# Fewer unread decay products, one wait more on GpSimd, and other places for the gated stage's guests

## The chip, the cores and the metric

The kernel runs on one core of a Trainium2 chip. The metric is the device time in microseconds (us) of one execution. TensorE (PE) multiplies matrices, VectorE (DVE), ScalarE (ACT) and GpSimd (POOL) work element by element, and SyncE (SP) issues DMAs. Each engine runs its instructions in order, and engines wait for each other by semaphores.

## What is computed

Four layers over 16 batches of 256 tokens with 128 channels. Each adds `layernorm(f(layernorm(x)))` to x:

```
x = x + _layernorm(_L0_attn_ref(_layernorm(x), ...))   # softmax attention, 16 heads of 8
x = x + _layernorm(_L0_ffn_ref(_layernorm(x), ...))    # attention, then 8 experts (top 2) and a shared one
x = x + _layernorm(_L1_attn_ref(_layernorm(x), W))     # power attention with decay
x = x + _layernorm(_L1_ffn_ref(_layernorm(x), ...))    # 7 capped experts
```

In the second layer a token's output is the shared expert's plus two chosen experts', each weighted. The third is the one with the decay:

```
log_G = jnp.cumsum(jax.nn.log_sigmoid(...), axis=1)
Tm = DEG * jnp.log(jnp.abs(S) + EPS) + jnp.log(jnp.float32(scale))   # DEG = 2
Z = Tm + log_G[..., :, None] - log_G[..., None, :]
P = jnp.exp(Z - Z_rowmax);  O = P @ V;  y = O / sum(P)
```

## The kernel before

Four stages run one after the other in one program: softmax attention (twice, up to about 500 us of the span), the gated experts (500 to 668), the power attention (668 to 955) and the capped experts with their routing (955 to 1102).

**The gated stage** (`gated_layer`) goes over 62 units n of 256 rows; `ORDER` says which unit is one of the shared expert (16 of them) and which is of rows sorted by expert (46). For a unit PE computes the gate and up products (`ggate_ps`, `gup_ps`, L2346), ACT the silu of the gate (`gsg`, L2430), DVE the product of both (`gprod`, L2645), and PE, one to four units later, the down product (`gdown_ps`, L2318). DVE adds a shared unit's result to XB (`add_shared`, L2573); ACT copies a sorted one's to `gob` (L2399), and SP stores it to DRAM (`mixed`). `down` for unit x waits, because `gdown_ps` has two banks, until unit x-2 was taken (`released`). `finished(kind, n)` lists the units whose result DVE or ACT takes at step n, ahead of the product; `DOWNS` lists the down products that PE makes at steps 4 and 5.

GpSimd scatters rows to their sorted places (L2175) by 32 indirect DMAs for the second half of the rows, waits for stores, and gathers results back (`ggot`, L2187) by 8 indirect DMAs for each block of 512 tokens; there are 8 blocks b. A block then passes through `add0` and `add1` (4 DVE instructions each, L2586, which weigh the gathered rows into XB), `moments` (L2598, L2602, L2603), a root on GpSimd (`out_root`, L2193, at the places in `ROOTS`), `shift` (L2607), `rows` on ACT (4 activations, L2405; `first` and `second` are two of them each), and `added` (L2613), the sum into X. Two dictionaries from step to calls, the guests, say after which unit each engine does these; the first work of the power stage (T, QK, V, CS for batches 0 and 1, `moments`, `gates`, `rows`, `softplus`) stands in the same dictionaries. `s_sum` counts finished additions, two a block, and `gated.EARLY` is 6.

**The power stage** (`power_layer`) goes over steps t, one for each batch and then some to run out, with 8 units u in each; n = 8t + u. For a unit PE fills a bank with decays (`decay_ps`, from `late` and then from M, L1560) and score banks (L1564, L1578), DVE takes the score's absolute value (`A`, L1419), ACT takes exp of the decay (`E`, L1235) and the square of A (`PT`, L1223), GpSimd multiplies both in `PT` (`multiply`, L993) two units later, and PE multiplies by V (L1597). E has 4 buffers, so ACT's exp of unit n waits for the multiply of n-4. The order on every engine is written out by (t, u). In `decays`, L1543 starts the accumulation; the products of L1542 before it go to the same bank, and L1543 (start=True) overwrites them, so nobody reads them. There is one of them in each unit for t < 10, none for t from 10 to 13, and two for t = 14 and 15.

Blocks 4 to 7 are gathered and added while the power stage begins: `add0(4)` at (0, 1), `add1(4)` at (0, 3), `add0(5)` at (0, 7), `add1(5)` at (1, 0). ACT waits for `s_sum` of 12 before the square of unit 9.

Of the kernel before, what the change touches and what calls it, by code (L numbers as in the profile page):

```python
# [41 lines left out]
NB, S, D = 16, 256, 128  # L42
# [791 lines left out]
def power_layer(nc, low, weighted_in, top, take, X, cst, cstb, QK, Vx, w, Y, chosen, router, bias, yd, wi, wo, gated, dram):  # L834
# [7 lines left out]
    with ExitStack() as ctx:  # L842
# [235 lines left out]
        def gpsimd(pool, guests):  # L1078
# [432 lines left out]
        def tensor(pe, guests):  # L1511
# [92 lines left out]
            for t in STEPS:  # L1604
                for u in range(NU):
                    n = NU * t + u
# [378 lines left out]
def gated_layer(nc, big, small, temps, got_late, hTf, sg, prod, take, X, XB, cst, split, down_w, norm, lg, soft,  # L1985
# [33 lines left out]
    def turned_at(n):  # L2019
        kind, i = ORDER[n]  # L2020
        return turn_of(n) if kind == "sorted" or i % 2 == 0 else None

    with ExitStack() as ctx:
# [616 lines left out]
        def vector(dve, guests):  # L2640
# [333 lines left out]
def build(nc, dram, out):  # L2974
    with ExitStack() as ctx:
# [21 lines left out]
        with ExitStack() as c1:  # L2997
# [54 lines left out]
            def _(pool):  # L3052
# [25 lines left out]
                gated.gpsimd(pool, {**{("fixed", k): guest("fixed", k) for k in range(7)},  # L3078
                                    ("gather", 2, 2): several(guest("root", 0), guest("norm0", 0), guest("norm1", 0)),
                                    ("gather", 2, 7): guest("root", 1),  # L3080
                                    ("gather", 3, 1): several(guest("norm0", 1), guest("norm1", 1)),
                                    "end": several(guest("root", 2), guest("norm0", 2), guest("norm1", 2))})
# [10 lines left out]
            def _(act):  # L3093
# [9 lines left out]
                def rows(b):  # L3103
                    return lambda: gated.tail_scalar(act, "rows", b)

                def several(*calls):
                    return lambda: [call() for call in calls]
# [4 lines left out]
                soft.scalar(act, heads)  # L3112
                gated.scalar(act, {39: rows(0), 45: rows(1), 49: rows(2), 44: guest("T", 0), 46: guest("QK", 0),
                                   48: guest("V", 0), 50: guest("T", 1), 52: guest("QK", 1),
                                   54: several(guest("V", 1), guest("softplus", 0)), 56: guest("CS", 0),
                                   57: rows(3), 59: guest("CS", 1)})
                def half(part, b):
                    return lambda: gated.tail_scalar(act, part, b)

                after = {(0, 0): guest("factors", 0), (1, 0): rows(4)}  # L3120
# [5 lines left out]
            def _(dve):  # L3126
# [9 lines left out]
                def several(*calls):  # L3136
# [8 lines left out]
                soft.vector(dve, heads)  # L3145
                gated.vector(dve, {36: tail(("add0", 0)), 37: tail(("add1", 0), ("moments", 0)), 39: tail(("shift", 0)),
                                   40: several(tail(("added", 0)), guest("moments", 0)), 41: tail(("add0", 1)),
                                   42: tail(("add1", 1), ("moments", 1)), 43: guest("moments", 1), 44: tail(("shift", 1)),
                                   45: tail(("added", 1)), 46: several(guest("QK", 0), guest("moments", 2)),
                                   47: tail(("add0", 2)), 48: tail(("add1", 2), ("moments", 2)), 49: tail(("shift", 2)),  # L3150
                                   50: tail(("added", 2)), 51: tail(("add0", 3)), 52: guest("QK", 1),
                                   53: tail(("add1", 3), ("moments", 3)), 55: guest("gates", 0), 56: tail(("shift", 3)),
                                   57: several(guest("rows", 0), guest("gates", 1)),
                                   58: tail(("added", 3)), 59: guest("rows", 1),
                                   61: tail(("shared", gated.UNITS - 3))})
                after = {(0, 0): tail(("shared", gated.UNITS - 2)), (0, 1): tail(("add0", 4)),
# [57 lines left out]
```

## Time and profile before

| | us |
|---|---|
| median of 3 runs (lowest, highest) | 1105.17 (1102.54, 1108.28) |
| profiled execution, its own time | 1104.22 |
| its span, first to last instruction | 1102.3 |
| busy: PE / DVE / ACT / POOL | 992.7 / 850.8 / 774.9 / 637.9 |
| mean granted TensorE clock, share of full | 0.962 |

A busy share is an average over four stages with different limits. PE is listed busy from a matmul's start to its modelled end, so two pipelined matmuls overlap in it.

### The profile page before, as it was taken

To read this page: it belongs to the slowest core of one execution; us is meant where nothing else is said; L and a number is where in the kernel's file an instruction comes from. 1 tells how busy PE (TensorE), PEld (TensorE's weight loads), DVE (VectorE), ACT (ScalarE), POOL (GpSimd) and SP (SyncE) were. 2 spreads that over 40 slices of the span, in tenths; PEclk is the share of its full clock that TensorE was granted. 3 is DMA by queue.
4 is the path that set the end of the run, shared out by engine and by line. 5 is a ranking of instruction groups with operands and counts; after the bars stand their busy time and mean duration, and the time that the engine had idled before them with its cause. 6 is when DMAs were issued, how large, how long until landed. Compare 5 with 4: busy or idle time off the path is not lost. (4 is left out here: it accounts for less than half of the span.)

```text
span 1102.3 us, 30949 instructions
## 1 busy us (share of the span) xinstructions
PE 992.7 (90%) x10503; PEld 586.9 (53%) x10503; DVE 850.8 (77%) x2252; ACT 774.9 (70%) x1760; POOL 637.9 (58%) x710
## 2 busy tenths in 40 slices
PE   4899999999999988988999998999999999848975
PEld 2344444444444443436998875555555565534752
DVE  3789999999999998954756767888989987772324
ACT  1578888888888877884554665788888998642405
POOL 4235544555443333760476838799888887526753
PEclk9999999999999999998999998999999999858988
DMA  5022222211111111220444421112121121141227
GB/s 133 26 58 77 77 73 77 77 55 40 41 41 40 41 33 43 59 70 20 132 124 132 134 75 41 48 43 66 44 61 32 36 58 52 40 164 41 53 74 198
DMA packets 114423, 75.24 MB, mean 68 GB/s; under 512 B 21335, under 2 KB 107808, under 8 KB 114272
## 3 DMA queue, kind: packets, MB, share of 16 engines
q1 hardware_dynamic: 105840, 54.68, 18.2%
q0 software_dynamic: 7744, 18.13, 5.5%
q8 instruction: 90, 1.47, 0.6%
q14 instruction: 61, 0.50, 0.2%
q10 hardware_dynamic: 688, 0.46, 0.1%
HBM read 26.75 MB, written 26.51 MB: 48 GB/s over the span
## 5 line engine op out<-in xcount | busy, mean ns | idle before, releaser
L637 DVE TENSOR_REDUCE mxsS<-scoreS 128x2 f32<-128x512 f32 x512 | 327.7, 685 | 40.9 <-PE scoreS L779 37.2
L519 ACT ACTIVATE PTS<-stS 128x512 f32<-128x512 f32 x512 | 284.1, 595 | 55.4 <-PE stS L783 54.2
L779 PE MATMUL scoreS<-QK 31*128 31x256 f16 x1024 | 171.6, 280 | 30.6 <-DVE mxsS L637 16.5
L993 POOL TENSOR_TENSOR PTP<-PTP,EP 128x512 f32<-128x512 f32 x128 | 163.3, 1280 | 38.7 <-ACT PTP L1223 37.7
L783 PE MATMUL stS<-QK 32*128 32x256 f16 x1024 | 169.4, 278 | 2.3 <-ACT PTS L519 2.3
L701 PE MATMUL pvS<-PTS,Vx 128*32 128x256 f32 x2048 | 142.0, 396 | 0.4 <-ACT PTS L519 0.2
L779 PEld LDWEIGHTS scoreS<-QK 31*128 31x128 f16 x1024 | 52.7, 93 | 152.6 <-DVE mxsS L637 105.5
L1419 DVE TENSOR_SCALAR AP<-score_psP 128x768 int32<-128x768 int32 x128 | 121.7, 951 | 12.1 <-PE score_psP L1578 10.6
L1223 ACT ACTIVATE PTP<-AP,epsP 128x768 f32<-128x768 f32 x128 | 118.9, 929 | 6.8 <-DVE AP L1419 6.5
L392 POOL TENSOR_TENSOR rsS<-veS,halfS 128x2 f32<-128x2 f32 (+1 forms) x32 | 33.0, 1031 | 154.0 <-DVE veS L605 87.1
L1235 ACT ACTIVATE EP<-decay_psP 128x512 f32<-128x512 f32 x128 | 75.7, 592 | 29.1 <-PE decay_psP L1560 27.4
L2175 POOL DMA_INDIRECT sorted<-gy,gidx x64 | 62.0, 969 | 41.5 <-DVE gowner L2537 22.8
L701 PEld LDWEIGHTS pvS<-PTS,Vx 128*32 128x32 f32 x2048 | 54.5, 111 | 51.0 <-issue 23.0
L2318 PE MATMUL gdown_ps<-down_w,gprod 128*128 (+1 forms) x496 | 65.7, 276 | 3.4 <-DVE XB L2573 3.1
L2318 PEld LDWEIGHTS gdown_ps<-down_w,gprod 128*128 128x128 f32 x496 | 60.1, 192 | 5.3 <-issue 4.4
L2645 DVE TENSOR_TENSOR gprod<-gsg,gup_ps 128x512 f32<-128x512 f32 x62 | 42.5, 686 | 22.2 <-ACT gsg L2430 10.9
L2187 POOL DMA_INDIRECT ggot<-mixed,gidx x48 | 46.7, 973 | 21.7 <-issue 13.3
L2367 ACT ACTIVATE ghTs<-gturn_ps,norm 128x256 f16<-128x256 f32 x46 | 21.8, 473 | 50.3 <-PE gturn_ps L2257 49.5
L783 PEld LDWEIGHTS stS<-QK 32*128 32x128 f16 x1024 | 51.9, 93 | 6.2 <-ACT PTS L519 3.1
L1560 PEld LDWEIGHTS decay_psP<-MP 32*128 32x128 bf16 x512 | 28.5, 93 | 48.6 <-issue 44.1
L398 POOL TENSOR_SCALAR yS<-X,mvS,rsS 128x128 f32<-128x128 f32 x64 | 50.6, 797 | 1.7
L1564 PE MATMUL score_psP<-QK 31*128 31x128 f16 x512 | 50.6, 218 | 0.0
(399 smaller groups left out, 2310.7 us busy)
## 6 DMA issues: line engine op xcount, KB each, us to landing
QK<-HLS SPq DMA_DIRECT2D x384, 32.0 KB
QK<-HLP SPq DMA_DIRECT2D x192, 32.0 KB
gsin<-sorted SPq DMA_DIRECT2D x46, 128.0 KB
mixed<-gob SPq DMA_DIRECT2D x46, 128.0 KB
sorted<-ggot POOLq DMA_DIRECT2D x22, 256.0 KB, 2.7
expert_outputs<-tzero SPq DMA_DIRECT2D x8, 512.0 KB
cgot<-expert_outputs SPq DMA_DIRECT2D x16, 256.0 KB, 5.4
tokens<-XB SPq DMA_DIRECT2D x16, 128.0 KB
```

The costliest lines, as they stand in the source:

```text
L398: last = pool.tensor_scalar(y[:, c, :], rows_of(X, b)[c], mv[:, c, 0:1], rs[:, kind, c:c + 1], ALU.subtract, ALU.mult)
L519: act.activation(PT[:, n % NPT, :], st_ps[:, (NS * t + n) % 3, :], ACT.Exp, scale=SCALE).then_inc(s_exp, 1)
L637: dve.tensor_reduce(mxs[:, u // 4, :, at], score_ps[:, n % 2, :].rearrange("p (c s) -> p c s", c=TC), AX.X, ALU.max).then_inc(s_max, 1)
L701: last = pe.matmul(pv_ps[32 * j:32 * j + 32, q], Vx[:, t % 3, c, 4 * g + j, :], PT[:, (4 * g + (j ^ 2)) % NPT, S * c:S * c + S], start=(c ...
L779: scored = pe.matmul(score_ps[:, k, cols], QK[part, new, g, 0, rows], QK[part, new, g, 1, :], start=True, stop=True)
L783: turned = pe.matmul(st_ps[:, (NS * t + n) % 3, cols], QK[part, old, g, 1, rows], QK[part, old, g, 0, :], start=True, stop=True)
L993: eng.tensor_tensor(w, w, E[:, n % NE, :], ALU.mult).then_inc(s_wd if n % NU in MULT_BY_DVE else s_wp, 1)
L1223: act.activation(PT[:, n % NW, :], A[:, n % NA, :], ACT.Square, bias=eps[:, 0:1]).then_inc(s_sq, 1)
L1235: act.activation(E[:, n % NE, :], decay_ps[:, n % 2, :], ACT.Exp).then_inc(s_taken, 1)
L1419: dve.tensor_scalar(A[:, n % NA, :].bitcast(I32), score_ps[:, n % 2 * WU:n % 2 * WU + WU].bitcast(I32), 0x7FFFFFFF, None, ALU.bitwise_and) ...
L2175: pool.indirect_dma_start(tables[h], bass.IndirectOffsetOnAxis(ap=idx[h][:, c, t:t + 1], axis=0), y[:, tiles[h].start + t, :], None).then_ ...
L2318: last = pe.matmul(down_ps[:, x % 2, t * D:(t + 1) * D], prod[:, x % NPROD, c * SLOTS + t * P:c * SLOTS + (t + 1) * P], down_flat[:, colum ...
```

## The change

It does four things. In the power stage the unread product remains in steps 0 and 1 (one) and 15 (two), and goes in steps 2 to 9 (one in each of 64 units) and 14 (two in each of 8). GpSimd waits at (1, 0), ahead of its multiply of unit 6, until `s_sum` is 12. In the gated stage units 0 to 3 are taken by DVE right behind the products of units 4 and 5 instead of ahead of those of 5 and 6. And the guests of units 35 to 61, with GpSimd's order of fixed rows, scatters, gathers and roots, are laid out anew.

```
@@ power_layer, gpsimd
                 for u in range(NU):
                     n = NU * t + u - 2
+                    if (t, u) == (1, 0):
+                        pool.wait_ge(gated.s_sum, 2 * gated.EARLY)
                     if 0 <= n < NU * NB and n % NU not in MULT_BY_DVE:
                         multiply(pool, n)
@@ power_layer, decays
-                for _ in range(AGAIN if t >= NB - 2 else t < 10):
+                for _ in range(AGAIN if t == END else t < 2):
                     pe.matmul(decay_ps[:, n % 2, :], cstb[:, 0:P], late, start=True, stop=True)
@@ gated_layer
-        ROOTS = ((1, 4), (2, 6), (3, 6))
+        ROOTS = ((1, 6), (2, 7), (3, 7))
         def gpsimd(pool, guests):
             scaled_rows(pool, NBLK - 1)
+            for k in range(7):
+                guests["fixed", k]()
             for k in range(2 * len(tiles[1])):
                 scatter(pool, 1, k)
-            for k in range(7):
-                guests["fixed", k]()
...
-            return [x for x in ({5: (0, 1), 6: (2, 3)}.get(n, (n - 3,) if n > 6 else ())) if ORDER[x][0] == kind]
+            return [n - 3] if n > 6 and ORDER[n - 3][0] == kind else []
...
                 product(n)
+                for x in DOWNS.get(n, ()):
+                    add_shared(dve, x)
@@ build, scalar
-                gated.scalar(act, {39: rows(0), 45: rows(1), 49: rows(2), 44: guest("T", 0), 46: guest("QK", 0),
...
-                                   57: rows(3), 59: guest("CS", 1)})
+                gated.scalar(act, {39: half("first", 0), 40: half("second", 0), 44: guest("T", 0), 45: half("first", 1),
...
+                                   56: guest("CS", 0), 58: half("first", 3), 59: guest("CS", 1), 60: half("second", 3)})
@@ build, vector
-                gated.vector(dve, {36: tail(("add0", 0)), 37: tail(("add1", 0), ("moments", 0)), 39: tail(("shift", 0)),
...
-                                   53: tail(("add1", 3), ("moments", 3)), 55: guest("gates", 0), 56: tail(("shift", 3)),
+                gated.vector(dve, {35: tail(("add0", 0)), 36: tail(("add1", 0)), 37: tail(("moments", 0)),
...
+                                   55: several(guest("gates", 0), tail(("added", 2))), 56: tail(("moments", 3)),
```

ACT's halves stand at units 39 and 40, 45 and 46, 53 and 55, 58 and 60. On GpSimd the guests of the power stage move from (gather, 2, 2), (2, 7) and (3, 1) to (2, 5) and (3, 2).

DVE, gated stage, from the product of unit 4. Before (`gprod` the product, `ghTs` the low half of a later unit's rows, `gm` to `gone` the first four steps of choosing experts, `XB<-gdown_ps` two shared units added):

```order
L2645 TENSOR_TENSOR gprod<-gsg,gup_ps 128x512
L2450 SCALAR_TENSOR_TENSOR ghTs<-gturn_ps,norm,ghTs 128x256
L2482 TENSOR_REDUCE gm<-lg 128x16
L2483 TENSOR_TENSOR gpr_121<-lg,gm 128x128
L2484 SCALAR_TENSOR_TENSOR gsc<-gpr_121,cst 128x128
L2485 TENSOR_REDUCE gone<-gsc 128x16
L2573 SCALAR_TENSOR_TENSOR XB<-gdown_ps,XB 128x256 x2
L2645 TENSOR_TENSOR gprod<-gsg,gup_ps 128x512
```

And after:

```order
L2647 TENSOR_TENSOR gprod<-gsg,gup_ps 128x512
L2575 SCALAR_TENSOR_TENSOR XB<-gdown_ps,XB 128x256 x2
L2452 SCALAR_TENSOR_TENSOR ghTs<-gturn_ps,norm,ghTs 128x256
L2484 TENSOR_REDUCE gm<-lg 128x16
L2485 TENSOR_TENSOR gpr_121<-lg,gm 128x128
L2486 SCALAR_TENSOR_TENSOR gsc<-gpr_121,cst 128x128
L2487 TENSOR_REDUCE gone<-gsc 128x16
L2647 TENSOR_TENSOR gprod<-gsg,gup_ps 128x512
```

The two additions moved up past five instructions; the same holds one unit later.

DVE, gated stage, block 0 behind the product of unit 36. Before:

```order
L2586 SCALAR_TENSOR_TENSOR XB<-ggot,gW,XB 128x128 x4
L2645 TENSOR_TENSOR gprod<-gsg,gup_ps 128x512
L2450 SCALAR_TENSOR_TENSOR ghTs<-gturn_ps,norm,ghTs 128x256
L2586 SCALAR_TENSOR_TENSOR XB<-ggot,gW,XB 128x128 x4
L2598 BN_STATS gstats<-XB 128x6 x4
L2602 BN_AGGR gmv<-gstats 128x2 x4
L2603 TENSOR_SCALAR gve<-gmv 128x4
L2645 TENSOR_TENSOR gprod<-gsg,gup_ps 128x512
```

And after, from the first additions, now behind unit 35:

```order
L2588 SCALAR_TENSOR_TENSOR XB<-ggot,gW,XB 128x128 x4
L2647 TENSOR_TENSOR gprod<-gsg,gup_ps 128x512
L2452 SCALAR_TENSOR_TENSOR ghTs<-gturn_ps,norm,ghTs 128x256
L2588 SCALAR_TENSOR_TENSOR XB<-ggot,gW,XB 128x128 x4
L2647 TENSOR_TENSOR gprod<-gsg,gup_ps 128x512
L2452 SCALAR_TENSOR_TENSOR ghTs<-gturn_ps,norm,ghTs 128x256
L2600 BN_STATS gstats<-XB 128x6 x4
L2604 BN_AGGR gmv<-gstats 128x2 x4
L2605 TENSOR_SCALAR gve<-gmv 128x4
L2647 TENSOR_TENSOR gprod<-gsg,gup_ps 128x512
```

A product now stands between the second additions and the moments.

GpSimd, gated stage, from the last scaled rows (`MP`, `VkP`: fixed rows of the power stage; `grs`: root of a block; `rsP`, `yP`: guests of the power stage). Before:

```order
L2175 DMA sorted<-gy,gidx_109 5888x128 x32
L1054 CAST MP<-cst 128x4x256 x4
L1058 MEMSET VkP 128x3x256 x2
L2187 DMA ggot<-mixed,gidx_108 128x128 x13
L2193 TENSOR_TENSOR grs<-gve,ghalf 128x4
L2187 DMA ggot<-mixed,gidx_108 128x128 x6
```

And after:

```order
L1054 CAST MP<-cst 128x4x256 x4
L1058 MEMSET VkP 128x3x256 x2
L2177 DMA sorted<-gy,gidx_109 5888x128 x32
L2189 DMA ggot<-mixed,gidx_108 128x128 x15
L2195 TENSOR_TENSOR grs<-gve,ghalf 128x4
L2189 DMA ggot<-mixed,gidx_108 128x128 x7
```

The fixed rows moved ahead of the scatters, and block 0's root behind two more gathers.

## Rows read from the trace of the kernel before

**Rows 1.** Windows, power stage: stretch and length, busy us (count), clock, DMA.

```profile
670.80:692.40 21.60, 16.60 (x164) 8.38 (x166) 18.16 (x41) 13.36 (x24) 18.13 (x17) 0.84 0.14 37
...
726.50:743.80 17.30, 16.98 (x223) 9.46 (x224) 16.27 (x47) 15.29 (x35) 16.16 (x17) 1.00 0.20 50
762.10:781.00 18.90, 18.45 (x238) 10.35 (x238) 17.18 (x47) 15.99 (x35) 16.63 (x16) 1.00 0.21 53
798.40:816.70 18.30, 17.69 (x229) 10.09 (x228) 15.56 (x40) 16.60 (x39) 17.19 (x16) 1.00 0.22 57
...
852.90:870.10 17.20, 15.92 (x221) 9.95 (x220) 15.82 (x40) 16.19 (x38) 14.56 (x15) 1.00 0.13 34
870.10:886.30 16.20, 16.09 (x221) 9.95 (x220) 14.66 (x40) 14.79 (x35) 13.10 (x13) 1.00 0.14 36
...
918.90:936.40 17.50, 17.50 (x227) 9.48 (x228) 13.88 (x33) 13.51 (x27) 12.32 (x11) 1.00 0.22 62
```

**Rows 2.** Source view of L1419: count, ns min/median/max, first and last start.

```profile
L1419 DVE TENSOR_SCALAR AP<-score_psP x128: 935/950/959, 670.8 to 950.7; 128x768 int32<-128x768 int32 x128
```

**Rows 3.** Timeline of PE, step 1: start us, us, engine line op.

```profile
701.40 0.39 PE L1542 MATMUL decay_psP<-cstb 128*128 128x512 bf16 x1
701.62 0.38 PE L1543 MATMUL decay_psP<-cstb 128*128 128x512 bf16 x1
```

**Rows 4.** Timeline of PE, gated units 4 to 7: idle before in brackets.

```profile
511.32 1.95 PE L2318 MATMUL gdown_ps<-down_w,gprod 128*128 128x128 f32 x16
...
516.29 2.02 PE L2318 MATMUL gdown_ps<-down_w,gprod 128*128 128x128 f32 x16 [1.49 <-DVE XB L2573]
...
521.43 1.15 PE L2318 MATMUL gdown_ps<-down_w,gprod 128*128 x8 [1.59 <-DVE XB L2573]
```

**Rows 5.** Timeline of DVE, gated unit 4 to the product of unit 5.

```profile
512.51 0.69 DVE L2645 TENSOR_TENSOR gprod<-gsg,gup_ps 128x512 f32<-128x512 f32 x1 [0.85 <-PE gdown_ps L2318]
...
515.72 0.76 DVE L2573 SCALAR_TENSOR_TENSOR XB<-gdown_ps,XB 128x256 f32<-128x256 f32 x2
```

**Rows 6.** Source view of L2645 in two windows, 584:597 and 596.4:648.

```profile
L2645 DVE TENSOR_TENSOR gprod<-gsg,gup_ps x6: 686/689/689, 584.4 to 596.5; 128x512 f32<-128x512 f32 x6
...
L2645 DVE TENSOR_TENSOR gprod<-gsg,gup_ps x19: 677/686/690, 596.5 to 647.8; 128x512 f32<-128x512 f32 x19
```

**Rows 7.** Timeline, gated stage: a product of DVE, ACT's rows of block 0.

```profile
637.46 0.69 DVE L2645 TENSOR_TENSOR gprod<-gsg,gup_ps 128x512 f32<-128x512 f32 x1 [2.46 <-ACT gsg L2430]
...
606.15 1.65 ACT L2405 ACTIVATE gtmp<-XB,gnm,grs 128x128 f32<-128x128 f32 x4 [0.62 <-DVE gnm L2607]
```

**Rows 8.** Timeline of GpSimd, gated stage and its end.

```profile
536.09 1.06 POOL L2175 DMA_INDIRECT sorted<-gy,gidx  x1 [22.82 <-DVE gowner L2537]
...
576.42 3.98 POOL L1054 CAST MP<-cst 128x1024 bf16<-128x1024 f32 x4
...
647.90 1.03 POOL L2193 TENSOR_TENSOR grs<-gve,ghalf 128x4 f32<-128x4 f32 x1 [9.46 <-DVE gve L2603]
656.73 1.10 POOL L2187 DMA_INDIRECT ggot<-mixed,gidx  x1 [7.80 <-DMA mixed<-gob]
...
676.62 2.50 POOL L993 TENSOR_TENSOR PTP<-PTP,EP 128x512 f32<-128x512 f32 x2
...
689.73 1.27 POOL L993 TENSOR_TENSOR PTP<-PTP,EP 128x512 f32<-128x512 f32 x1
```

**Rows 9.** Timeline of DVE, steps 0 and 1: the additions of blocks 4 and 5.

```profile
673.20 1.13 DVE L2586 SCALAR_TENSOR_TENSOR XB<-ggot,gW,XB 128x128 f32<-128x128 f32 x4
...
676.93 4.78 DVE L2586 SCALAR_TENSOR_TENSOR XB<-ggot,gW,XB 128x128 f32<-128x128 f32 x4
...
693.28 1.46 DVE L2586 SCALAR_TENSOR_TENSOR XB<-ggot,gW,XB 128x128 f32<-128x128 f32 x4
```

**Rows 10.** Timeline of ACT, exp of units 4 and 10.

```profile
677.99 0.60 ACT L1235 ACTIVATE EP<-decay_psP 128x512 f32<-128x512 f32 x1 [0.74 <-POOL PTP L993]
...
695.38 0.58 ACT L1235 ACTIVATE EP<-decay_psP 128x512 f32<-128x512 f32 x1
```

More of the change, by code:

```diff
@@ L3078, in _ @@
                 gated.gpsimd(pool, {**{("fixed", k): guest("fixed", k) for k in range(7)},
-                                    ("gather", 2, 2): several(guest("root", 0), guest("norm0", 0), guest("norm1", 0)),
-                                    ("gather", 2, 7): guest("root", 1),
-                                    ("gather", 3, 1): several(guest("norm0", 1), guest("norm1", 1)),
+                                    ("gather", 2, 5): several(guest("root", 0), guest("norm0", 0), guest("norm1", 0)),
+                                    ("gather", 3, 2): several(guest("root", 1), guest("norm0", 1), guest("norm1", 1)),
                                     "end": several(guest("root", 2), guest("norm0", 2), guest("norm1", 2))})
@@ L3104, in rows, with half @@
                     return lambda: gated.tail_scalar(act, "rows", b)
+                def half(part, b):
+                    return lambda: gated.tail_scalar(act, part, b)
                 def several(*calls):
@@ L3112, in _ @@
                 soft.scalar(act, heads)
-                gated.scalar(act, {39: rows(0), 45: rows(1), 49: rows(2), 44: guest("T", 0), 46: guest("QK", 0),
-                                   48: guest("V", 0), 50: guest("T", 1), 52: guest("QK", 1),
-                                   54: several(guest("V", 1), guest("softplus", 0)), 56: guest("CS", 0),
-                                   57: rows(3), 59: guest("CS", 1)})
-                def half(part, b):
-                    return lambda: gated.tail_scalar(act, part, b)
+                gated.scalar(act, {39: half("first", 0), 40: half("second", 0), 44: guest("T", 0), 45: half("first", 1),
+                                   46: several(half("second", 1), guest("QK", 0)), 48: guest("V", 0), 50: guest("T", 1),
+                                   52: guest("QK", 1), 53: half("first", 2),
+                                   54: several(guest("V", 1), guest("softplus", 0)), 55: half("second", 2),
+                                   56: guest("CS", 0), 58: half("first", 3), 59: guest("CS", 1), 60: half("second", 3)})
                 after = {(0, 0): guest("factors", 0), (1, 0): rows(4)}
@@ L3145, in _ @@
                 soft.vector(dve, heads)
-                gated.vector(dve, {36: tail(("add0", 0)), 37: tail(("add1", 0), ("moments", 0)), 39: tail(("shift", 0)),
[L3147 to L3151, printed above, removed]
-                                   53: tail(("add1", 3), ("moments", 3)), 55: guest("gates", 0), 56: tail(("shift", 3)),
-                                   57: several(guest("rows", 0), guest("gates", 1)),
-                                   58: tail(("added", 3)), 59: guest("rows", 1),
-                                   61: tail(("shared", gated.UNITS - 3))})
+                gated.vector(dve, {35: tail(("add0", 0)), 36: tail(("add1", 0)), 37: tail(("moments", 0)),
+                                   38: tail(("shift", 0)), 39: tail(("add0", 1)), 40: tail(("added", 0)), 41: guest("moments", 0),
+                                   42: tail(("add1", 1)), 43: tail(("moments", 1)),
+                                   44: tail(("shift", 1)), 45: guest("moments", 1), 46: guest("QK", 0),
+                                   47: tail(("added", 1)), 48: guest("moments", 2), 49: tail(("add0", 2)),
+                                   50: tail(("add1", 2)), 51: tail(("moments", 2)), 52: guest("QK", 1),
+                                   53: tail(("shift", 2), ("add0", 3)), 54: tail(("add1", 3)),
+                                   55: several(guest("gates", 0), tail(("added", 2))), 56: tail(("moments", 3)),
+                                   57: several(guest("rows", 0), guest("gates", 1), tail(("shift", 3))),
+                                   59: guest("rows", 1),
+                                   61: tail(("added", 3), ("shared", gated.UNITS - 3))})
                 after = {(0, 0): tail(("shared", gated.UNITS - 2)), (0, 1): tail(("add0", 4)),
```

## The prediction

> **What bounds the kernel now.** I read the windows by stage first, then the waits of each engine in the stages that the change touches, then the timelines at the waits that ended last. The chain of waits at the kernel's end lies in the capped experts, behind all of this; what is gained ahead of it moves it as a whole, so each stage is read for itself.
>
> In the power stage I cut the windows at the start of every eighth L1419, so that one window is one step; there are 128 of them from 670.8 to 950.7 us [rows 2]. A step takes 16.2 to 18.9 us. PE is listed busy for nearly all of it (16.09 of 16.20 in step 11), but DVE and ACT are close: in step 3 DVE has 16.27 of 17.30, in step 5 17.18 of 18.90 [rows 1]. PE holds most units, DVE those in which it has additions or moments to do besides. A microsecond taken from PE is thus worth less than one.
>
> In the gated stage DVE's products show the pace: 5 units from 584.4 to 596.5, 2.42 us each, with PE busy all the time, then 18 units from 596.5 to 647.8, 2.85 us each [rows 6]. Two places lie outside that pace: PE idle 1.49 and 1.59 us in units 5 and 6 [rows 4].
>
> The power stage's first step takes 21.6 us at a clock of 0.84 [rows 1], because DVE, GpSimd and PE stumble over the last gathers.
>
> **The unread products.** 64 + 16 = 80 matmuls go. One costs PE 0.22 us from its start to the next [rows 3], so 17.6 us if PE were all that counts: one end. The other is nothing, if DVE and ACT hold every unit. Steps with and without one stand in the same trace. Step 7 (one a unit) and step 10 (none) have the same work beside it, the second half of a block's rows on ACT and its sum on DVE, except for two gathers on GpSimd: 18.3 against 17.2 us [rows 1], 1.1 for the 1.8 us of PE taken out. Steps 4 and 7: 2 x 1.1 = 2.2. Steps 3, 6 and 9 carry a block's moments: DVE has 16.27 in 17.30 [rows 1] against 14.66 in 16.20 in step 11, and step 11 shows that DVE loses 1.5 us a step to waits even without the product. 16.3 + 0.7 to 1.5 is 17.0 to 17.8, so the gain is 0.3 at most: 3 x 0.3 = 0.9. Steps 5 and 8 carry the additions: 17.18 of DVE and the 1.4 us that it waits in step 10 (17.20 less 15.82) give 18.6, against 18.9; with some of these waits gone, 18.2. I take 0.7 each, 1.4. Step 2 lies between these kinds: 0.5. Step 14 loses two a unit: 17.5 against 16.2 in step 11, though DVE has less to do in it (13.88 against 14.66) [rows 1]; I take 1.1. Sum 6.1; by bounds 2.5 (only steps 4, 7 and part of 14) to 9.
>
> **Units 4 to 6 of the gated stage.** The down products of units 0 and 1 run on PE from 511.32 to 513.27 [rows 4]. DVE could add them then, but its product of unit 4 ends at 513.2 and four steps of choosing follow; the additions come at 515.72 [rows 5]. PE has to wait for them with its next down product, until 516.29, and once more until 521.43 [rows 4]. After the change the additions follow the product: 513.3 to 514.0, before PE asks: its wait of 1.49 us ended at 516.29, so it asked at 514.8. For units 2 and 3 the product of unit 5 now no longer waits for 0.76 us of additions, and PE asks about 3 us later. Both waits go: 3.1. What is late next is DVE itself: its chain of choosing ends the ranks, and the first scatter waits for it 22.82 us [rows 8]; it moves up with PE, as does everything that PE paces up to unit 35.
>
> Against it stands what GpSimd now does in the same time. The fixed rows, with 3.98 us of CAST [rows 8], run from 513.3 on, not at 576.4. In the trace two of DVE's instructions with two SBUF operands, of the four in one addition, stretched under GpSimd's multiplies, 4.78 for 1.13 us [rows 9]; the CASTs have one operand, and no row has such a DVE instruction beside them. If they block, up to four of choosing's instructions wait until about 517.4, and of the 3.1 us 1.2 are left. If not, 3.1. I take 2.6, nearer to the row without any hold. The fixed rows' own 5.4 us cost nothing in the idle 22.82, and gain nothing: the gathers behind them wait for stores that PE paces.
>
> The Trainium skill says of this (SBUF — State Buffer, section "SBUF: two separate sides") that VectorE and GpSimd share a port pair as an exclusive lock, also for a VectorE instruction with two SBUF inputs against any GpSimd instruction that reads SBUF. By that the CASTs block and the term would be 1.2; the 4.78 us agree with the lock, and no run here shows it for a CAST.
>
> **The guests of units 35 to 61.** 18 units took 51.3 us, and at the pace ahead of them 43.6. The power stage's T, QK and V for two batches are PE's own work; from their durations I estimate 2.2 us a set, 4.3 for both. So 3.4 us are lost where guests bunch: DVE's product waits 2.46 us for ACT (one of two such waits), behind four of ACT's rows, 1.65 us in one piece [rows 7]. Halves and one kind of guest a unit break that up. All of it is 3.4, nothing is 0, and worse is possible in units 53 to 60, where ACT gets 0.8 us in 53 and again in 55, beside the softplus: up to 1 us lost. I take 2.0, a little over the middle.
>
> **The entry to the power stage.** Block 3's moments go from unit 53 to 56, so its root on GpSimd, at 647.90 before, comes after them, by this count at about 657 to 659 in the old times. The 16 gathers of blocks 4 and 5 stand behind it; they began at 656.73, held by a store, and the first multiply came right behind them at 676.62 [rows 8]. They begin 1 to 3.5 us later. ACT's exp of unit 4 already waited 0.74 us for that multiply [rows 10], so this lands on the path, up to 3.5. In return the additions of block 4, which took 4.78 instead of 1.13 us under the multiplies [rows 9], may get through before them: up to 3.6 back. The new wait holds the multiply of unit 6, at 689.73 before [rows 8], until block 5's additions end at 693.28 + 1.46 = 694.7 [rows 9]: 5 us. Behind it on GpSimd stand the multiplies of 7 and 8 and a gather; ACT's exp of unit 10 waits for the held multiply, which would end at 696.0, 0.6 us later than the exp began [rows 10]. With GpSimd late already, the wait costs less. Together between 3 gained and 4 lost; I take 0.7 lost.
>
> **Sum.** 6.1 + 2.6 + 2.0 - 0.7 = 10.0 us, from the profiled execution's 1104.2: 1094.2. That execution lies 0.95 under the median of the runs (1105.17), within their scatter; I give 1094.5.
>
> **Rivals.** First, *DVE holds the steps*. Steps 3, 5, 6, 8 and 9 give nothing, and waits for DVE take PE's place: 2.5 instead of 6.1. For it: DVE's 16.3 of 17.3 us. Against: the 1.1 us between steps 7 and 10, both with additional work. Time 1098.1.
>
> Second, *GpSimd comes late*. The root behind unit 56 puts the gathers 3.5 us back, none of DVE's blocking goes, and the wait in step 1 is paid in full: 4 lost at the entry, 1097.5. For it: the multiply right behind the gathers, and exp waiting for it. Against: E's four buffers, and that most of the 4.78 was blocking.
>
> Third, on the other side, *the clock falls*. PE's clock was at its upper level (2.4 GHz) in the windows from step 2 on, and its mean in step 0, where PE waited long for DVE, 0.84 [rows 1]. Without the unread products PE has less to do in steps held by DVE, most of all 5 and 8. At 1.2 GHz the 16.1 us of PE in a step become 32, so one step costs 16 us: from 0.6 of a step on the gain is used up, and with one the time is 1110. Against: steps 10 to 13 have none of them and kept 1.00, step 10 with 15.92 of 17.20 [rows 1]. The Trainium skill has the rule behind it (TensorE: Matmul & The Clock Gate, Part 1): the throttled state is the default, and activity releases it.
>
> **Chances.** Forecast 0.62, DVE 0.14, GpSimd late 0.15, clock 0.05, the rest 0.04 for the gated stage's layout turning out worse (1100). What a measurement of this kernel tells from no change is about 0.5%, 5.5 us: faster means under 1099.6. Of the forecast nearly all lies there, of the first two rivals some three quarters: 0.61 + 0.11 + 0.11 = 0.83, which I lower to 0.80 for what I don't see; same 0.14, slower 0.06. The range, 1088.5 to 1100.5, reaches at the upper end past both milder rivals and at the lower to bounds of 9, 3.1, 3.4 and nothing lost.
>
> **What would show it.** In the profile after: step windows 4 and 7 at 17.2 to 17.4, 14 at 16.2 to 16.5, and 3, 6, 9 at about 17 with DVE the engine waited for; clock 1.00 in all of them. No wait of `gdown_ps` for XB in units 5 and 6, and unit 14's product some 2.6 us earlier. Under 2.75 us a unit from 36 to 54. The first gather of block 4 one to three us behind the store that it waited for, and GpSimd idle ahead of the multiply of unit 6. Wrong would be steps 4 and 7 above 18, a clock under 1.00 in steps 2 to 14, or a first step above 24 us.

## The result

The changed kernel took 1110.32 us in the median of 19 runs (1102.86 to 1114.67, and one of 1452.34 us at a granted clock of 0.559, which the comparison leaves out), the kernel before 1104.00 beside it (19 runs). The ratio is 1.004, 95% interval 1.0023 to 1.0056: some 4 us slower (the two medians lie 6.3 us apart), where the prediction had said 10 faster. The profiled execution took 1113.14 us, 3 above the median, span 1111.2, mean granted TensorE clock 0.940 where it was 0.962.

The steps of the power stage tell where the time went. Windows of the kernel after, one step each (0, 1, 2, 3, 4, 5, 6, 7, 8, 9, and 14); columns as in [rows 1]:

```profile
668.60:688.50 19.90, 16.22 (x173) 8.29 (x172) 16.56 (x42) 13.09 (x24) 17.83 (x17) 0.91 0.17 45
688.50:709.00 20.50, 19.51 (x188) 10.29 (x188) 14.46 (x32) 14.89 (x31) 16.38 (x14) 0.75 0.10 26
709.00:724.30 15.30, 15.20 (x215) 9.30 (x214) 13.85 (x34) 13.79 (x30) 14.23 (x14) 1.00 0.22 56
724.30:744.20 19.90, 18.27 (x215) 10.96 (x214) 16.32 (x49) 16.27 (x36) 18.47 (x18) 0.83 0.20 50
744.20:761.40 17.20, 15.97 (x221) 9.92 (x220) 15.75 (x39) 15.60 (x36) 15.29 (x15) 1.00 0.20 50
761.40:781.00 19.60, 17.93 (x256) 11.00 (x255) 18.84 (x48) 16.94 (x37) 18.57 (x17) 1.00 0.23 58
781.00:801.50 20.50, 18.75 (x186) 11.18 (x186) 16.47 (x49) 14.63 (x33) 14.30 (x14) 0.75 0.17 46
801.50:820.30 18.80, 17.55 (x221) 11.08 (x220) 15.99 (x41) 16.65 (x39) 17.73 (x17) 0.91 0.22 56
820.30:839.90 19.60, 17.96 (x256) 11.02 (x255) 18.83 (x48) 16.70 (x36) 15.49 (x14) 1.00 0.18 45
839.90:863.90 24.00, 22.96 (x186) 13.45 (x186) 16.79 (x49) 15.63 (x35) 13.63 (x13) 0.57 0.10 25
...
929.80:945.20 15.40, 14.47 (x213) 8.62 (x213) 13.69 (x33) 13.87 (x28) 11.92 (x12) 1.00 0.27 75
```

Against [rows 1], step 4 shortened as forecast (17.2), and step 14 by more (17.5 to 15.4). But steps 3, 6, 7 and 9 ran partly at TensorE's lower level (1.2 GHz): a mean of 0.57 over 24.0 us means 20.6 us at half. Steps 2 to 9 took 154.9 us, before 143.1; PE starts fewer matmuls and is listed busy longer (step 3: 215 for 223, 18.27 us for 16.98 [rows 1]). And steps 5 and 8, which kept 1.00, got longer without their product: 19.6 us where step 5 took 18.9 [rows 1], with 18.84 us of DVE for 17.18.

Why is seen at the end of step 5. Timelines of the kernel after there, of DVE, GpSimd and PE:

```profile
778.48 0.17 DVE L1312 SCALAR_TENSOR_TENSOR lgP<-misc_aP,geP 128x32 f32<-128x32 f32 x1
778.58 2.51 DVE L2588 SCALAR_TENSOR_TENSOR XB<-ggot_late,gW,XB 128x128 f32<-128x128 f32 x2
781.01 0.94 DVE L1421 TENSOR_SCALAR AP<-score_psP 128x768 int32<-128x768 int32 x1
```

```profile
778.38 2.55 POOL L993 TENSOR_TENSOR PTP<-PTP,EP 128x512 f32<-128x512 f32 x2
```

```profile
782.01 0.28 PE L1580 MATMUL score_psP<-QK 31*128 31x128 f16 x2 [1.77 <-DVE AP L1421]
```

The same place in the kernel before, DVE and GpSimd:

```profile
780.13 0.92 DVE L2586 SCALAR_TENSOR_TENSOR XB<-ggot_late,gW,XB 128x128 f32<-128x128 f32 x2
```

```profile
779.36 1.28 POOL L993 TENSOR_TENSOR PTP<-PTP,EP 128x512 f32<-128x512 f32 x1
781.04 1.28 POOL L993 TENSOR_TENSOR PTP<-PTP,EP 128x512 f32<-128x512 f32 x1 [0.40 <-ACT PTP L1223]
```

With the product PE set the pace, and ACT's squares came 0.4 us late to GpSimd. In that gap DVE's two additions got through: they met only the end of the first multiply and took 0.92 us. Without the product the multiplies run back to back, the additions lie under them and take 2.51, DVE's next pass over the scores is late, PE waits 1.77 us for it, and the next window is the one at 0.75 (behind step 8: 0.57).

The parts ahead of the power stage came about as forecast. In the kernel after, PE's down products of units 4 to 6 don't wait, where they waited 1.49 and 1.59 us [rows 4]:

```profile
512.91 1.95 PE L2320 MATMUL gdown_ps<-down_w,gprod 128*128 128x128 f32 x16
...
516.22 1.95 PE L2320 MATMUL gdown_ps<-down_w,gprod 128*128 128x128 f32 x16
...
519.73 1.15 PE L2320 MATMUL gdown_ps<-down_w,gprod 128*128 x8
```

and the source view of DVE's products from unit 36 to 54 answers to [rows 6]:

```profile
L2647 DVE TENSOR_TENSOR gprod<-gsg,gup_ps x19: 675/686/689, 595.8 to 644.9; 128x512 f32<-128x512 f32 x19
```

49.1 us for 18 units, 2.73 each, before 2.85.

### The profile page after: what moved, and what is told of

Read it like the earlier page. It is cut to its first block and busy times, and to the rows that moved or that the text cites. A ratio compares the mean times of both kernels' runs of the same rounds, so it can differ in the third digit from the quotient of the medians.

```text
span 1111.2 us, 30790 instructions
## 1 busy us (share of the span) xinstructions
PE 996.3 (90%) x10423; PEld 596.5 (54%) x10423; DVE 853.1 (77%) x2252; ACT 776.2 (70%) x1760; POOL 637.5 (57%) x710
## 5 line engine op out<-in xcount | busy, mean ns | idle before, releaser
L1566 PE MATMUL score_psP<-QK 31*128 31x128 f16 x512 | 53.0, 226 | 0.0
L1562 PE MATMUL decay_psP<-MP 32*128 32x128 bf16 x512 | 53.0, 226 | 0.0
L1545 PE MATMUL decay_psP<-cstb 128*128 128x512 bf16 x128 | 52.7, 412 | 0.0
```

The costliest lines, as they stand in the source:

```text
L1562: decay = pe.matmul(decay_ps[:, n % 2, o:o + P], M[band, t % 2, g, 1, rows], M[band, t % 2, g, 0, rows], start=False, stop=(k == 1 and c = ...
```

## The experiments

All ran beside the kernel before, whose median stayed between 1103.9 and 1105.5; ratios are to it, with their 95% intervals. A ratio is not the quotient of the two medians; the two ways differ by up to 2.5 us, so differences of 2 us between experiments say little. "Wait theory" in the expectations stands for a fall of the clock set off by single waits of PE, "load theory" for one set off by too little work in a step. "Kept in" and "gone in" speak of the steps that have the unread product, which nobody reads: no output depends on it.

**Products and layout apart.** Four kernels: the kernel before with the condition

```
-                for _ in range(AGAIN if t >= NB - 2 else t < 10):
+                for _ in range(AGAIN if t == END else t < 2):
```

and nothing else (e1); the changed kernel without that line (e2); and the same two with step 14's products alone gone (e3, e4: `AGAIN if t == END else t < 10`).

> The kernel before with the unread products alone taken out (steps 2 to 9 and 14). Clock theory (without them PE's clock falls in steps that DVE holds): the granted clock falls in two or more of steps 3, 6, 9, these steps take 19.5 to 24 us in place of 17.3, mean clock 0.94 to 0.955, ratio 1.004 to 1.012. Rival (the slower time comes from the new GpSimd wait and the late root, not from the products): no fall after step 1, steps 4 and 7 at 17.3, ratio 0.993 to 0.997.

> The changed kernel with the unread products as before, so only the gated stage's layout and the GpSimd wait are new. Clock theory: no fall of the clock from step 2 to 14, first product of the power stage some 3.5 us earlier, ratio 0.993 to 0.998. Rival (GpSimd wait and late root): steps 0 and 1 together 2 us or more longer than the 38.9 of before, ratio 1.002 to 1.006.

> The kernel before with the products of step 14 alone taken out (steps 0 to 9 keep one a unit). Clock theory: no DVE-held step is touched, so no fall, step 14 at 15.5 to 16.3 in place of 17.4, ratio 0.998 to 0.9995. Rival (any unread product keeps the clock up): a fall in step 14 or 15, step 14 over 18, ratio over 1.001.

> The changed kernel with the products kept in steps 0 to 9 and gone only in step 14. Clock theory: gains of the gated stage and of step 14 add, ratio 0.991 to 0.997. Rival (GpSimd wait): ratio 1.000 to 1.005.

Measured: e1 1118.06 us, 1.0104 [1.0069, 1.0140]; e2 1097.23, 0.9932 [0.9901, 0.9962]; e3 1101.56, 0.9972 [0.9948, 0.9996]; e4 1097.50, 0.9926 [0.9898, 0.9955]. All four ratios lie where the clock theory had them (e3 a little below); but e2 and e3 have a fall of 3.4 us in step 10, where the expectation of e2 had none. So the products' removal costs 11 to 12 us in either layout (13 by the medians), and the rest of the change gains 7.5. Windows of e1, steps 5 and 6, in which nothing but the products differs from before:

```profile
757.90:777.50 19.60, 17.95 (x256) 11.00 (x255) 18.84 (x48) 16.94 (x37) 18.57 (x17) 1.00 0.23 58
777.50:801.50 24.00, 22.98 (x186) 13.49 (x186) 16.68 (x49) 15.73 (x35) 15.68 (x15) 0.57 0.16 43
```

and the same steps in e2:

```profile
753.00:771.90 18.90, 18.45 (x238) 10.35 (x238) 17.16 (x47) 15.99 (x35) 16.61 (x16) 1.00 0.20 55
771.90:789.20 17.30, 16.99 (x223) 9.80 (x220) 16.29 (x49) 15.00 (x34) 15.64 (x15) 1.00 0.21 55
```

**Is it the wait, or too little work?** In e10 all products stay, and DVE does its first pass for units 48 and 72 (first of steps 6 and 9) three times (arguments of the calls left out below). e9, e5 and e6 are the kernel before with products gone in two or three steps (`t < 10 and t not in (5, 8)` and so on).

```
+                        for k in range(2 if n in (48, 72) else 0):
+                            dve.tensor_scalar(A[:, n % NA, :].bitcast(I32), ...).then_inc(s_twice, 1)
+                            dve.wait_ge(s_twice, 2 * (n // 72) + k + 1)
                         dve.tensor_scalar(A[:, n % NA, :].bitcast(I32), ...).then_inc(s_abs, 1)
```

> The kernel before with all its unread products, and VectorE's first pass over the scores of the first unit of steps 6 and 9 done three times in place of once, the first two read by nobody: a wait of about 1.6 us for TensorE at the start of these two steps, made by nothing else. Wait theory in its strict form (a wait alone does it): the clock falls to half behind both for 10 to 20 us, ratio 1.008 to 1.015. If it takes the wait and steps that are short of work together: the clock stays, 2 x 1.9 us more, ratio 1.003 to 1.004.

> The kernel before, the unread product left out in steps 5 and 8 alone. Wait theory: in both, VectorE's two additions into XB behind lgP come to lie under GpSimd's multiply (1.23 and 1.36 us for 0.66 and 0.34), the step is 19.6 us for 18.9, TensorE waits 1.77 us at the start of the next, and the granted clock falls to half there though steps 6 and 9 have their products: 0.7 and about 6 us more, each twice, ratio 1.008 to 1.013. Load theory: the additions and the wait are there, but steps 6 and 9 with their products keep the clock: 1.4 us more, ratio 0.999 to 1.003.

> The kernel before, the unread product left out in steps 2, 4 and 7 alone. Wait theory: the clock is held at half only where TensorE has just waited 1.2 us or more in front of a far score for VectorE's first pass; in these steps the only such waits are of 1.2 us (steps 4 and 7, as with the products all gone), none longer, so no long fall. The steps shorten as in the run with the products gone, 16.8 to 15.4, 18.3 to 17.3 and 18.3 to 17.3: 3.5 us less, ratio 0.996 to 0.999. Load theory (TensorE has too little work in a step without the product, wherever it is): a fall in or behind each of the three, ratio 1.003 to 1.01.

> The kernel before, the unread product left out in steps 3, 6 and 9 alone, the steps that showed 20 us at half clock when it was gone everywhere. Wait theory: the waits of 1.77 us at the start of steps 6 and 9 come from the step ahead of each (5 and 8, which keep their product here), so they don't occur and steps 6 and 9 stay at full clock, 16.9 to 17.4 us; step 3 may keep a wait of 1.26 us and a fall of 3.4 us (+1.5 us). Ratio 0.998 to 1.002. Load theory: steps 6 and 9 run at half clock for 20 us again, 6.6 us more each, ratio 1.008 to 1.013.

e10: 1116.21 us, 1.0126 [1.0096, 1.0156], 14 us for two waits (12 by the medians). In its profile steps 5 and 8, at whose ends the waits stand, took 2 us more each, and steps 6 and 9, at the lower clock, 2.7 and 5.6 more. Timeline of PE at the two places, and windows of the steps they stand in (6 and 9):

```profile
782.13 0.22 PE L1584 MATMUL score_psP<-QK 31*128 31x128 f16 x1 [1.69 <-DVE AP L1425]
...
841.38 0.28 PE L1584 MATMUL score_psP<-QK 31*128 31x128 f16 x2 [1.67 <-DVE AP L1425]
```

```profile
781.10:801.20 20.10, 18.69 (x193) 10.51 (x194) 16.71 (x48) 14.41 (x34) 14.00 (x15) 0.83 0.16 45
...
840.40:863.30 22.90, 21.53 (x192) 11.57 (x192) 16.59 (x48) 14.66 (x33) 12.31 (x12) 0.70 0.08 21
```

With every product in place a wait of 1.7 us was followed by the fall, both times: a wait alone is enough. e9: 1106.20, 1.0009 [0.9984, 1.0033]. Its windows of steps 8 and 9, and PE at the start of step 9:

```profile
818.60:838.20 19.60, 18.31 (x257) 11.01 (x256) 18.84 (x48) 16.79 (x36) 16.23 (x15) 1.00 0.19 51
838.20:855.40 17.20, 15.77 (x192) 9.03 (x192) 16.19 (x49) 14.39 (x33) 12.31 (x12) 1.00 0.11 29
```

```profile
839.17 0.22 PE L1578 MATMUL score_psP<-QK 31*128 31x128 f16 x1 [1.35 <-DVE AP L1419]
```

The additions are stretched again (18.84 of DVE), but two of step 9's own products stand on PE ahead of that score (at 834.06 and 835.73) and fill 0.4 of the 1.77 us; with 1.35 left the clock held. A fall of 3.4 us stood in step 5, behind waits of only 0.42 and 0.48 us. Here my expectation of a fall missed, and the number is that of the load theory; e10 shows that full steps don't hold the clock against a wait of 1.7 us, but the fall in step 5 has no such wait. e5: 1101.62, 0.9971 [0.9955, 0.9988]; steps 2, 4 and 7 at 15.6, 17.5 and 17.5 us, clock 1.00, as the wait theory had it. e6: 1100.69, 0.9971 [0.9948, 0.9994], no fall in its three steps (17.3, 17.2 and 17.2 us); in its profile steps 2 to 9 together shorten by 0.6, so its measured gain of 3 us is larger than its steps account for.

**Only steps 5 and 8 put back.** e11 is the changed kernel, e14 the kernel before, both with this condition (in e14 the last step is written `NB - 1`, the same)

```
+                for _ in range(AGAIN if t == END else t < 2 or t in (5, 8)):
```

> The changed kernel, its unread product put back in steps 5 and 8 alone (so in steps 0, 1, 5, 8 and 15). Theory (a wait of TensorE of about 1.7 us sets off the fall, stretched additions of steps 5 and 8 make the wait): the additions are 0.66 and 0.34 us again, no wait above 1.4 us stands between steps 3 and 9, no fall of 10 us or more between them; the time is that of the kernel with products kept but in 14 (1097.5) less about 3 us, 1094, ratio 0.988 to 0.992. Rival (too few products as such): falls stay in steps 3, 6, 7 and 9 and the ratio is 1.000 or more.

> The kernel before with the products of the changed kernel and those of steps 5 and 8 as well; nothing moved. Against the run with the products gone in 2 to 9 and 14 (1.0104) it differs by the 16 products of steps 5 and 8 alone. Theory as for the run above: 0.988 to 0.994, 15 to 20 us under it with 16 instructions more. Rival (too few products as such): 1.005 or more.

e11: 1099.42, 0.9943 [0.9921, 0.9964]; e14: 1103.78, 0.9986 [0.9962, 1.0009]. Against e1 (1.0104) e14 issues 16 matmuls more and is about 13 us quicker. DVE's additions at the end of step 5 in e11, and its windows of steps 3, 5, 6, 8 and 9:

```profile
772.04 0.93 DVE L2588 SCALAR_TENSOR_TENSOR XB<-ggot_late,gW,XB 128x128 f32<-128x128 f32 x2
```

```profile
716.60:736.60 20.00, 18.24 (x216) 11.04 (x215) 16.76 (x50) 16.22 (x36) 18.67 (x18) 0.83 0.19 50
754.00:772.90 18.90, 18.45 (x240) 10.54 (x239) 17.16 (x47) 16.26 (x37) 16.89 (x16) 1.00 0.23 56
772.90:791.30 18.40, 16.84 (x211) 10.67 (x210) 15.81 (x50) 15.54 (x36) 16.80 (x16) 0.91 0.23 58
810.70:832.00 21.30, 20.86 (x240) 11.29 (x240) 17.25 (x47) 15.59 (x36) 14.00 (x13) 0.87 0.15 39
832.00:849.20 17.20, 15.48 (x211) 9.51 (x210) 16.20 (x50) 14.70 (x34) 13.58 (x13) 1.00 0.13 32
```

The additions are back at 0.93 and the falls of 20 us are gone. But shorter ones stay, of 6.8 and 10.2 us by PE's waits of 1.38 (step 3) and 1.23 us (step 7), and one of 3.4 in step 6 behind a wait of only 0.80: the forecast of 0.988 to 0.992 was too good. So was that of e14, 0.988 to 0.994: its profile has falls of 13.7 us from step 3 on and three of 3.4, in steps 4, 6 and 9. Of the rival it is true that falls stay, but not its time.

**Which steps can be without.** The changed kernel with products gone in 4, 7 and 14 (e15), in 4, 6, 7, 9 and 14 (e18), and kept to step 10 (e17); conditions `t < 10 and t not in (4, 7)`, `t < 4 or t in (5, 8)`, `t < 11`.

> The changed kernel with the unread product left out in steps 4, 7 and 14 alone. Steps 4 and 7 are held by TensorE, and without their product they took 17.3 to 17.5 us for 18.3 with waits of 1.15 to 1.23 us. Wait theory (only waits of some 1.5 us and more reliably set off a fall): no fall of 6 us or more between steps 2 and 9, and 1.7 to 2.0 us less than with 14 alone (0.9926): ratio 0.990 to 0.992. Load theory: a fall in or behind steps 4 and 7 gives it back: 0.993 to 0.996.

> The changed kernel with the unread product left out in steps 4, 6, 7, 9 and 14: against the run with only 5 and 8 put back (0.9943) it keeps steps 2 and 3 as well. Wait theory: the wait of 1.3 us in step 3 and its 6.8 us at half clock (step 3 19.9 for 17.3) need steps 2 and 3 both without products, so they go; steps 6 and 9 may still show a fall of 3.4 us. 2.6 us less and 1.5 more for step 2: ratio 0.991 to 0.994. Load theory: falls remain in steps 6, 7 and 9 and nothing is won, 0.994 to 0.997.

> The changed kernel with its unread product in steps 0 to 10 and 15, so in step 10 as well, which had none in any kernel so far and in most profiled executions shows a wait of 1.22 us and 3.4 us at half clock (18.7 us for 17.3). Wait theory: the products fill the time, the wait goes, the step takes 17.3 us with its clock full in every execution: 1 us under the kernel that has them in 0 to 9 and 15 (0.9926), ratio 0.991 to 0.993. Rival (the products only take TensorE's time): 1 us above, 0.9935.

e15: 1098.33, 0.9926 [0.9887, 0.9964]. e18: 1098.32, 0.9927 [0.9899, 0.9955]. e17: 1098.55, 0.9950 [0.9926, 0.9975]. e18 came within its forecast; e15 and e17 came out above theirs, e15 with a fall of 3.4 us in step 7, and the intervals of both reach down into the forecast. No version is told from e4 (0.9926). Windows of e15, steps 4, 7 and 10, of e18, step 3, and of e17, step 10:

```profile
740.20:757.70 17.50, 16.26 (x222) 9.98 (x222) 16.07 (x41) 16.48 (x39) 16.88 (x17) 1.00 0.21 55
793.90:812.90 19.00, 17.78 (x222) 11.18 (x222) 16.04 (x40) 16.70 (x39) 17.66 (x17) 0.91 0.22 56
849.10:869.30 20.20, 18.90 (x221) 11.73 (x220) 15.96 (x40) 16.98 (x39) 15.67 (x15) 0.83 0.14 36
```

```profile
722.80:740.00 17.20, 16.88 (x222) 9.44 (x222) 16.19 (x47) 15.18 (x34) 16.19 (x16) 1.00 0.19 51
```

```profile
846.30:864.40 18.10, 17.49 (x228) 10.06 (x226) 15.50 (x40) 16.41 (x38) 14.94 (x14) 1.00 0.13 34
```

Steps 4 and 7 of e15 have nearly the same work; one kept its clock, the other lost 1.5 us, behind waits of 1.16 and 1.15. With steps 2 and 3 kept in e18, step 3's wait and fall are gone, as expected; falls of 3.4 us stay in steps 4, 6 and 9. In e17 a product in step 10 removes the wait of 1.22 us and the clock holds, but the step takes 0.8 us more than the 17.2 of [rows 1]: by the median it wins nothing.

**The entry and the CASTs.** e13 is e11 without GpSimd's new wait, e16 the kernel before with that wait alone, e12 e11 with the fixed rows back behind the scatters.

```
                     n = NU * t + u - 2
+                    if (t, u) == (1, 0):
+                        pool.wait_ge(gated.s_sum, 2 * gated.EARLY)
```

> The first kernel of this call without GpSimd's wait for the additions at the start of the second step. Theory: the wait costs 0.9 us of GpSimd's time and nothing of the end; without it the multiply of unit 6 and the last additions into XB share the time and stretch each other: within 1 us of the first kernel, ratio within 0.001 of it. Rival (the wait is what orders the entry): the additions take 2 us each again as in the kernel before, and TensorE waits over 3 us for them: 2 to 4 us more.

> The kernel before with one edit of the change: GpSimd's wait for the additions at the start of the second step. In the kernel before, the two long additions (2.34 and 1.93 us) lie under multiplies of the first step, ahead of this wait. Theory (the new places move that collision to the start of the second step and the wait then takes it away; neither does it alone): nothing, ratio 0.999 to 1.001. Rival (the wait alone brings the entry's gain): 0.996 to 0.998.

> The first kernel of this call, the seven fixed rows of guests back behind the scatters in GpSimd's program, so that their CASTs don't lie under VectorE's work for gated units 4 to 6. Port theory: VectorE's two operations over gpr and gsc take 0.29 us each again (0.74 and 1.00 in the changed kernel), and the gated stage is up to 1.2 us shorter: ratio 0 to 0.001 under the first kernel's. Rival: TensorE's waits for the down products of units 4 and 5 are back (1.5 us each), 2 to 3 us more, ratio 0.002 to 0.003 above it.

e13: 1103.03, 0.9991 [0.9968, 1.0013], so the wait is worth 4 to 5 us in the new layout (3.6 by the medians, 5.3 by the ratios), where I had said within 1. DVE's additions in steps 0 and 1 of e13, and PE behind them:

```profile
684.63 1.60 DVE L2586 SCALAR_TENSOR_TENSOR XB<-ggot,gW,XB 128x128 f32<-128x128 f32 x4
687.10 5.50 DVE L2586 SCALAR_TENSOR_TENSOR XB<-ggot,gW,XB 128x128 f32<-128x128 f32 x4
```

```profile
693.52 0.28 PE L1578 MATMUL score_psP<-QK 31*128 31x128 f16 x1 [3.84 <-DVE AP L1419]
```

The last four additions, 1.12 us in the kernel after, take 5.50 under the multiplies. e16: 1101.57, 0.9962 [0.9940, 0.9984], the rival's number: the wait gains by itself. GpSimd waits long for it there, and the step is none the longer (timeline of GpSimd and window of step 1 in e16; before, step 1 took 17.3):

```profile
694.20 2.97 POOL L993 TENSOR_TENSOR PTP<-PTP,EP 128x512 f32<-128x512 f32 x2 [4.36 <-DVE XB L2588]
```

```profile
692.10:708.80 16.70, 15.83 (x205) 8.77 (x198) 14.37 (x33) 14.45 (x31) 14.25 (x13) 1.00 0.13 33
```

That is 0.6 us; where can four come from (2.4 by the medians)? From executions that the profile of before doesn't show. Of the eight profiled executions whose entry is that of before, four (before, e1, e3, e10) took 38.7 to 39.0 us for steps 0 and 1, and four (e5, e6, e9, e14) 41.4 to 43.4. DVE and GpSimd at the end of step 0 in the kernel before:

```profile
692.34 0.16 DVE L2607 SCALAR_TENSOR_TENSOR gnm<-gmv,grs 128x4 f32<-128x4 f32 x1
```

```profile
692.48 1.27 POOL L993 TENSOR_TENSOR PTP<-PTP,EP 128x512 f32<-128x512 f32 x1 [1.47 <-ACT PTP L1223]
```

and in e6, with PE:

```profile
691.00 1.25 DVE L2607 SCALAR_TENSOR_TENSOR gnm<-gmv,grs 128x4 f32<-128x4 f32 x1
```

```profile
690.95 1.29 POOL L993 TENSOR_TENSOR PTP<-PTP,EP 128x512 f32<-128x512 f32 x1 [1.26 <-ACT PTP L1223]
```

```profile
693.18 0.28 PE L1578 MATMUL score_psP<-QK 31*128 31x128 f16 x2 [1.70 <-DVE AP L1419]
```

In before the small instruction began 0.14 us ahead of the multiply and took 0.16; in e6 it began 0.05 behind and took 1.25, until the multiply's end. PE then waited 1.70 us and step 1 ran at a mean clock of 0.75, 20.6 us long. All eight profiles divide by it: in the four short ones it began 0.07 to 0.14 us ahead and took 0.15 to 0.16, in the four long ones 0.02 to 0.06 behind and took 1.25 to 1.27, and PE waited 1.70 to 1.72. The new wait holds that multiply back, so this race is no longer run. That the executions without a profile divide in the same way is argued, not shown.

In the new layout another split remains, which the wait doesn't end. PE at the start of step 1 in the kernel after:

```profile
689.49 0.28 PE L1580 MATMUL score_psP<-QK 31*128 31x128 f16 x2 [1.74 <-DVE AP L1421]
```

In four of the eight executions with the new layout and the wait (after, e4, e17, e18) the fall of the clock in step 0 lasted 3.4 us, PE came early to this score, waited 1.54 to 1.86 us for DVE and fell to half again: 37.6 to 40.5 us for steps 0 and 1. In the other four (e2, e11, e12, e15) the fall in step 0 lasted 6.8 or 10.2 us, PE waited 0.7 at most, and the two steps took 36.4 to 38.0. So in the one profile of the kernel after the entry is 1.4 us longer than in before (40.3 for 38.9), though the medians of e2, e13 and e16 say that it gains. That PE waits because it is early is argued from these eight.

e12: 1099.64, 0.9942 [0.9919, 0.9965], the same as e11. The port theory's durations came: timeline of DVE, in the kernel after (with the CASTs of 4.10 us beside them from 514.90) and in e12:

```profile
516.33 0.74 DVE L2485 TENSOR_TENSOR gpr<-lg,gm 128x128 f32<-128x128 f32 x1
517.10 1.00 DVE L2486 SCALAR_TENSOR_TENSOR gsc<-gpr,cst 128x128 f32<-128x128 f32 x1
```

```profile
512.48 0.29 DVE L2485 TENSOR_TENSOR gpr<-lg,gm 128x128 f32<-128x128 f32 x1
512.80 0.29 DVE L2486 SCALAR_TENSOR_TENSOR gsc<-gpr,cst 128x128 f32<-128x128 f32 x1
```

but the 1.2 us gained there (from unit 0's product to unit 5's, against e11) had shrunk to 0.7 by unit 7, 0.6 by unit 36 and 0.3 by unit 61, and PE's down waits did not return: the earlier additions took those away, not the place of the fixed rows.

## Why the prediction was wrong

**The unread products** are the step that failed: forecast 6.1 gained, measured 11 to 12 lost (e1, e2 against after). The third rival came, which had 0.05. That its time, 1110, is the measured one is in part luck: it took one step of 32 us at the lower level, 16 us more. The profile of after has four shorter stretches between steps 2 and 9, 41 us in all, and they lengthened steps 3, 6, 7 and 9 by some 14 us together, a third of their length and not half (step 9: 6.6 us more for 20.5 at half clock). Two things were wrong in the step. First, steps 5 and 8 were given 0.7 us of gain each from a sum of DVE's busy time, 17.18 us, taken as fixed. It rose to 18.84, because the product's 0.2 us a unit was what kept DVE's additions clear of most of GpSimd's multiplies (e11 and e14 put it back, and the additions take 0.93 us again in e11); they cost 0.7 each instead. Second, I took the clock to hang on how busy PE is in a step, and held steps 10 to 13 against it. Step 10 was no safe witness: it has the same work in every kernel but e17, kept its clock in before and lost it for 3.4 or 6.8 us in six other profiles (e2, e3, e5, e6, e9, e15). By e10 a single wait is enough: in the 18 profiled executions (before, after and the 16 experiments) PE shows 15 waits of 1.5 us or more between the starts of steps 1 and 14, and behind 14 of them stands a stretch at half clock, 3.4 to 20.5 us long (the other stood in one already); of 35 waits of 1.15 to 1.24 us 12 have one, of 7 of 1.26 to 1.38 six. A hint stood in the trace of before: step 0 at 0.84 [rows 1], its fall 0.7 us behind a wait of PE for DVE of 3.48 us. I read that as an entry problem.

Had the clock held, the term would still have been smaller. By the steps' lengths at 1.00 in these runs, 2, 4 and 7 give 1.5, 1.0 and 1.0, step 14 2.0, steps 3, 6 and 9 nearly nothing and 5 and 8 minus 0.7 each: 4 us.

**Units 4 to 6.** Right, and partly by luck: forecast 2.6, from unit 0 to unit 7 2.9 us less (16.6 for 19.5), both waits gone. The CASTs do hold DVE, which I had thought the less likely and priced at 1.9 us, leaving 1.2. Without the hold (e12) the stretch takes 15.9: the gain was 3.6 and the hold cost 0.7 of it.

**The guests.** Right for their stretch: forecast 2.0, 2.2 us less between units 36 and 54, 2.73 us a unit, and DVE's two waits of 2.46 us for ACT are gone. But 0.7 us were given back between units 54 and 61, where the prediction had feared it, and as much between 7 and 36, so that the gated stage as a whole gained 3.7 (161.5 us from unit 0's product to the first step, before 165.2) and not 4.6.

**The entry.** Forecast 0.7 lost, and by the medians the sign was wrong. e2's 7.5 us less the gated stage's 3.7 leave 3.8 gained, in accord with e13 and e16; e2's own profile shows 2.5 of it in steps 0 and 1. The size of GpSimd's delay was read rightly as possible (4.36 us in e16), but nobody was waiting for it: what counted was DVE, whose last additions it no longer met. In the kernel after, the second additions of block 4 take 1.13 us where they took 4.78 [rows 9], by the new places and not by the wait, and the wait for the multiply of unit 6 is only 0.86 us. The root's shift (647.90 to 655.88) did put the gathers back: they began 11.5 us ahead of the first step, before 14.0 [rows 2, 8], 2.5 later as forecast. It cost nothing that shows, since step 0 took 19.9 us for 21.6.

On the port, the Trainium skill (SBUF — State Buffer, section "SBUF: two separate sides") says that a VectorE instruction with two SBUF inputs and a GpSimd instruction that reads SBUF exclude each other for a whole instruction. All rows above agree, the 1.25 us for 0.16 most plainly, and the case that no run had shown, a CAST, is now shown: 0.74 and 1.00 for 0.29.

**What stays open.** How far too little work adds to a wait. e6 shows waits of 0.8 us in steps 6 and 9 and no fall; e11, e12, e13, e14 and e18 show the same waits, and 8 of their 10 have a fall of 3.4 us beside them. They differ from e6 in lacking the products of other steps, so a share of the load theory stands, as it does by the fall in step 5 of e9; but e6 also ran on another chip than those five, and no run separates the two. And the falls' lengths differ from execution to execution of the same steps: behind the same wait of 1.26 us in step 3, 3.4 us in e1 and 13.7 in e14.

## What to carry to other kernels

A matmul that nobody reads can be worth more than its time, through the phase in which it sets other engines. Before it is removed, look at what lies beside what: list the DVE instructions with two SBUF operands and GpSimd's instructions that now just miss each other, and ask what a shift of half a microsecond does. Keep TensorE's single waits in a dense stage short; read the granted clock window by window behind each wait of a microsecond or more, and price a wait with the slowed work behind it (6 to 7 us for each 1.7 in e10). And a wait put on an engine that has time to spare, to keep it off another engine's instructions, can gain some microseconds (2 to 4 in e16) while the profile shows it as idle time (4.36 us). Where single profiles of one program differ, compare several before a stage's gain is read from one.

## What was not expected of the hardware

- Waits of TensorE of 1.67 to 1.77 us in a dense stage were each time, 11 of 11, followed by 7 to 20 us at 1.2 GHz (after, e1, e5, e6, e9, e10, e14); the one of 1.86 us in e17 by only 3.4.
- VectorE's smallest two-input instruction, 128x4 elements, took 1.25 us for 0.16 when it began 0.05 us behind a GpSimd multiply; the profiled executions split on such a margin, 38.7 to 39.0 us or 41.4 to 43.4 for the same two steps.
